# Mamba block, gated MLP and routed low-rank layer on one core: attention part moved forward in the step, norm rows turned by DMA, convolution read from PSUM

## The reference

```
h0  = LN(x)
a   = rmsnorm(h0) * ln1;  z, xBC, dt = a @ w_in.T
xBC = silu(causal depthwise conv of 4 taps over xBC + bias)        # x:128, B:128, C:4 x 128
dt  = softplus(dt + bias); chunks of 128 tokens, 4 heads: decayed scan (Mamba-2)
h1  = h0 + ((scan + D * x) * silu(z)) @ w_out.T
m   = h1 + (silu(h2 @ gate.T) * (h2 @ up.T)) @ down.T,  h2 = rmsnorm(h1) * ln2, 1792 inner channels
x1  = x + LN(m)
out = x1 + LN(u),  u = h3 @ W_up.T + low-rank term of the expert with the largest logit, h3 = LN(x1)
```

## Time and profile before

| | us |
|---|---|
| runs | 846.18, 846.56, 849.23; median 846.56 |
| profiled execution | 845.28, span 843.4 |
| PE busy, weight loads busy | 783.4 (93%), 552.9 (66%) |
| DVE, ACT, POOL busy | 488.4 (58%), 338.4 (40%), 148.7 (18%) |

### The profile page before, as it was taken

One profiled execution on the slowest core, in us unless ns is written; L12 is line 12 of the kernel. 1 busy time (PEld: TensorE's weight loads), 2 busy tenths in 40 slices (PEclk: granted clock), 3 DMA queues, 4 the chain that ended last, 5 costly groups with the idle time before them and its releaser, 6 DMA issues.

```text
span 843.4 us, 15200 instructions
## 1 busy us (share of the span) xinstructions
PE 783.4 (93%) x5712; PEld 552.9 (66%) x5726; DVE 488.4 (58%) x1123; ACT 338.4 (40%) x625; POOL 148.7 (18%) x198
## 2 busy tenths in 40 slices
PE   4987989899999999999999999999999999999944
PEld 3855855568657776678657776678656776677632
DVE  6877767676635764376635764476635764464343
ACT  2744667325522364225532364125532365122211
POOL 1412121012210141012210231012210231000000
PEclk9998999989999999999999999999999999999987
DMA  9930000000002000200002000200002000100010
GB/s 332 385 123 1 2 25 1 26 1 2 2 1 75 1 2 1 76 0 0 0 0 75 0 0 0 75 0 0 0 0 75 0 0 0 50 1 1 13 38 25
DMA packets 15556, 29.69 MB, mean 35 GB/s; under 512 B 1312, under 2 KB 1440, under 8 KB 15520
## 3 DMA queue, kind: packets, MB, share of 16 engines
q1 hardware_dynamic: 15520, 29.21, 9.8%
HBM read 25.01 MB, written 4.19 MB: 35 GB/s over the span
## 4 chain that ended last, share of the span: by engine, by line
PE 68%; issue 14%; DVE 9%; POOL 4%; ACT 3%; DMA 1%; SPq 0%; DVEq 0%; POOLq 0%; ACTq 0%
PE gu L1149 25%; PE wa L1149 21%; PE acc L1149 13%; PE wc L1149 6%; POOL y L411 2%; PE wa L1172 2%; DVE weights L806 1%; POOL ra L395 1%; DMA weights<-in_w_in 1%; DVE hn L835 1%; DVE weights L969 1%; DVE hn L843 1%; DVE sg L952 1%; DVE stats_a L821 1%; DVE h2t L946 1%
## 5 line engine op out<-in xcount | busy, mean ns | idle before, releaser
L1149 PE MATMUL gu<-h2t,weights 128*128 128x256 f16 x2688 | 314.6, 275 | 1.2 <-DVE h2t L946 1.2
L1149 PEld LDWEIGHTS gu<-h2t,weights 128*128 128x128 f16 x2688 | 261.8, 99 | 50.9 <-issue 15.0
L1149 PE MATMUL acc<-weights,act 128*128 128x512 f16 x672 | 164.6, 381 | 7.5 <-DVE act L957 7.5
L952 DVE SCALAR_TENSOR_TENSOR sg<-gu,bound,sg 128x256 f32<-128x256 f32 x112 | 53.6, 479 | 114.4 <-ACT sg L610 114.0
L610 ACT ACTIVATE sg<-gu,scale_inv 128x256 f32<-128x256 f32 x112 | 53.0, 473 | 150.1 <-PE gu L1149 150.0
L1149 PEld LDWEIGHTS acc<-weights,act 128*128 128x128 f16 x672 | 65.1, 98 | 65.2 <-DVE act L957 9.0
L620 ACT ACTIVATE act<-sg 128x256 f16<-128x256 f32 x112 | 46.6, 416 | 147.5 <-DVE sg L952 146.7
L1149 PE MATMUL wa<-ht,weights 128*128 128x256 f16 x912 | 105.7, 274 | 0.0
L1149 PEld LDWEIGHTS wa<-ht,weights 128*128 128x128 f16 x912 | 89.7, 98 | 16.9
L866 DVE SCALAR_TENSOR_TENSOR xbc<-conv_pad,conv_ws,xbc 128x256 f32<-128x256 f32 x144 | 67.2, 508 | 28.6 <-ACT conv_pad L545 19.2
L957 DVE TENSOR_TENSOR act<-sg,act 128x256 f16<-128x256 f32 x112 | 50.2, 448 | 54.8 <-ACT act L620 54.8
(11 more groups left out here) (189 smaller groups left out, 853.0 us busy)
## 6 DMA issues: line engine op xcount, KB each, us to landing
xa<-in_x SPq DMA_DIRECT2D x8, 512.0 KB, 3.5
weights<-in_x SPq DMA_DIRECT2D x8, 512.0 KB, 4.1
out_x<-h SPq DMA_DIRECT2D x16, 256.0 KB, 2.1
weights<-in_w_in SPq DMA_DIRECT2D x5, 512.0 KB, 6.7
weights<-in_w_down SPq DMA_DIRECT2D x3, 768.0 KB, 13.4
weights<-in_w_gate SPq DMA_DIRECT2D x2, 1024.0 KB, 11.9
weights<-in_w_up SPq DMA_DIRECT2D x2, 1024.0 KB, 13.8
weights<-in_w_gate SPq DMA_DIRECT2D x2, 768.0 KB, 14.3
```

The lines of the kernel that those rows point to most:

```text
L952: nc.vector.scalar_tensor_tensor(sg[:, f % 2], GU[f % 2][:, SEQ:2 * SEQ], up_to_act, sg[:, f % 2], ALU.mult, ALU.mult).then_inc(sem("prod_ ...
L1149: return nc.tensor.matmul(dst, left, right, start=start, stop=stop)
```

## The change

The tables are rewritten, so that part a starts earlier in its step. On PE:

```diff
-            A_AT = {1: lambda g: a_t1(g), 2: lambda g: a_in(g, 0), 3: lambda g: (a_in(g, 1), a_in(g, 2), a_dt(g)),
-                    4: lambda g: a_z(g, 0), 5: lambda g: (a_z(g, 1), a_tok(g)),
-                    6: lambda g: (a_dec(g, 0), a_dec(g, 1)), 7: lambda g: (a_att(g, 0), a_dec(g, 2)),
-                    8: lambda g: (a_att(g, 1), a_state(g)), 9: lambda g: (a_y(g, 0), a_y(g, 1)),
-                    10: lambda g: a_o(g, 0), 11: lambda g: a_o(g, 1), 13: lambda g: a_t2(g)}
-            C_AT = {4: lambda g: c_t3(g, 0), 5: lambda g: c_t3(g, 1), 6: lambda g: c_logits(g),
-                    7: lambda g: c_zt(g), 8: lambda g: c_u(g, 0), 9: lambda g: c_u(g, 1)}
+            A_AT = {0: lambda g: a_in(g, 1), 1: lambda g: (a_in(g, 2), a_dt(g)), 2: lambda g: a_z(g, 0),
+                    3: lambda g: (a_z(g, 1), a_tok(g)), 4: lambda g: (a_dec(g, 0), a_dec(g, 1)),
+                    5: lambda g: (a_att(g, 0), a_dec(g, 2)), 6: lambda g: (a_att(g, 1), a_state(g)),
+                    7: lambda g: (a_y(g, 0), a_y(g, 1)), 8: lambda g: a_o(g, 0), 9: lambda g: a_o(g, 1)}
+            NEXT_AT = {13: lambda g: a_in(g, 0)}
+            C_AT = {4: lambda g: alone(g) and (c_t3(g, 0), c_t3(g, 1)), 6: lambda g: c_logits(g),
+                    7: lambda g: c_zt(g), 10: lambda g: c_u(g, 0), 11: lambda g: c_u(g, 1)}
```

`NEXT_AT` holds work of the next group: its first input projection in block 13, on DVE its statistics, centring and lower half in blocks 8, 9 and 10, on ACT the upper half in block 10 and the first taps in block 13. On DVE:

```diff
-            A_AT = {1: lambda g: a_t1(g), 2: lambda g: a_conv(g, 0), 3: lambda g: (a_conv(g, 1), a_dtv(g)),
-                    4: lambda g: a_conv(g, 2), 5: lambda g: (a_dt(g), a_h0(g)),
...
+            A_AT = {0: lambda g: a_conv(g, 0), 1: lambda g: (a_conv(g, 1), a_dtv(g)),
+                    2: lambda g: (a_dt(g), a_conv(g, 2)), 3: lambda g: a_h0(g),
+                    5: lambda g: (a_dec(g, 0), a_dec(g, 1), a_att(g, 0)), 6: lambda g: a_att(g, 1),
+                    7: lambda g: (a_y(g, 0), a_y(g, 1)), 8: lambda g: a_h1(g, 0),
+                    9: lambda g: a_h1(g, 1), 10: lambda g: a_weight(g), 11: lambda g: a_lo2(g)}
+            NEXT_AT = {8: lambda g: a_stats(g), 9: lambda g: a_center(g), 10: lambda g: a_lo1(g)}
+            C_AT = {0: lambda g: c_stats1(g), 1: lambda g: c_x1(g), 3: lambda g: c_stats2(g), 4: lambda g: c_h3_lo3(g),
+                    6: lambda g: c_route(g), 12: lambda g: c_stats3(g), 13: lambda g: c_out(g)}
```

The three norms are no longer turned on PE, except those of group 0 and the last h3. ACT and DVE write f16 halves as rows, and SP turns them, 128 tokens with both halves (128x1024 f16, 256 KB) at a time, two transfers for each tensor:

```diff
+            def transposed(dst, rows, j, done):
+                sp.dma_start_transpose(dst[:, :, :, j * P:(j + 1) * P].rearrange("p s k q -> p (s k) q"),
+                                       rows[:, j].rearrange("p s d -> p (s d)")).then_inc(done, 16)
...
             def step(a, b, c):
+                following = a is not None and a + 1 < GROUPS
+                if following:
+                    a_x(a + 1)
+                if c is not None and not alone(c):
+                    c_t3(c)
+                if following:
+                    a_t1(a + 1)
+                if a is not None:
+                    a_t2(a)
                 if c is not None:
...
+                    c_store(c)
+                if b is not None:
+                    c_x(b)
+            a_x(1)
+            a_t1(1)
```

`h2t` becomes two tiles. The convolution's taps are read from PSUM, and ACT's copy to `conv_pad` goes away (group 0 keeps a copy for pairs 1 and 2):

```diff
-                            xbc[:, c], pad[:, c, k:k + SEQ], cw[:, c * TAPS + k:c * TAPS + k + 1],
-                            xbc[:, c], ALU.mult, ALU.add)
+                            xbc[:, c, late:], conv_in(g, c)[:, 0:SEQ - late], cw[:, c * TAPS + k:c * TAPS + k + 1],
+                            xbc[:, c, late:], ALU.mult, ALU.add)
```

So the PSUM banks rotate with the group, `a_z` waits for `conv_ready` of its pair, and `a_tok`, which writes over the third pair's products, waits for all six channel blocks:

```diff
             def a_tok(g):
                 pe.wait_ge(sem("xbc_ready"), g * 3 + 1)
-                pe.wait_ge(sem("dtv_ready"), g + 1)
+                pe.wait_ge(sem("conv_ready"), g * XBC + (2 if head(g) else XBC))
```

`wait_apart` is removed everywhere, and the hardware loop is replaced by steps written out:

```diff
-            with eng.Fori(2, GROUPS - 1) as i:
-                step(i + 1, i, i - 1)
...
+            for t in range(1, GROUPS + 2):
+                a, b, c = [g if 0 <= g < GROUPS else None for g in (t, t - 1, t - 2)]
+                step(a, b, c)
```

More of the change, by code:

```diff
@@ L169, in build @@
         ss = sb("sumsq", [P, 2, TILES])
-        h2t = sb("h2t", [P, 2, KB, SEQ], F16)
+        h2t = [sb(f"h2t_{n}", [P, 2, KB, SEQ], F16) for n in range(2)]
         h1b = sb("h1b", [P, TILES, D])
@@ L347, in _, with a_x, a_t1 @@
-            steps(sp, step)
+            def transposed(dst, rows, j, done):
+                sp.dma_start_transpose(dst[:, :, :, j * P:(j + 1) * P].rearrange("p s k q -> p (s k) q"),
+                                       rows[:, j].rearrange("p s d -> p (s d)")).then_inc(done, 16)
+            def a_x(g):
+                sp.wait_ge(sem("h0_ready"), g * 2)
+                sp.dma_start(xa[:], x_g[g]).then_inc(x_loaded, 16)
+            def a_t1(g):
+                sp.wait_ge(sem("z_ps_ready"), g * 2)
+                sp.wait_ge(sem("dt_ps_ready"), g)
+                for j in range(TILES):
+                    sp.wait_ge(sem("hn_split"), g * 2 + j - 1)
+                    transposed(ht, rows_1, j, ht_loaded)
@@ new lines, in a_t2, with c_x @@
+            def a_t2(g):
+                prev(g - 1, FBLK, FBLK, sp, sem("gu_ready"))
+                for j in range(TILES):
+                    sp.wait_ge(sem("h2_split"), g * 2 + j - 1)
+                    transposed(h2t[g % 2], rows_2, j, h2t_loaded)
+            def c_x(g):
+                if g > 0:
+                    sp.wait_ge(sem("out_ready"), g * 2)
+                if g == 0:
+                    wait_split(sp, order)
+                sp.dma_start(x1[:], x_g[g]).then_inc(xc_loaded, 16)
@@ L348, in _ @@
+            a_x(1)
+            a_t1(1)
+            steps(step)
             sp.wait_ge(stored, 16 * TILES * GROUPS)
@@ L483, in first @@
                 a_ce(0)
+                a_norm(1)
                 a_rms(0)
-                chain_a.close()
             first()
-            steps(pool, step)
+            steps(step)
         @block.scalar
@@ L621, in b_hi, with c_hi3 @@
                     .then_inc(sem("act_hi"), 1)
+            def c_hi3(g):
+                for j in range(TILES):
+                    eng.wait_ge(sem("h3_ready"), g * 2 + j + 1)
+                    nc.scalar.activation(rows_3[:, j, 0], h3[:, j], ACT.Copy).then_inc(sem("h3_hi"), 1)
             def c_t3(g, b):
-                eng.wait_ge(sem("h3t_ps_ready"), g * 2 + b + 1)
+                eng.wait_ge(sem("h3t_ps_ready"), b + 1)
                 prev(g, 2, 2, eng, sem("u_ps_ready"))
@@ L661, in step @@
                         C_AT[f](c)
+                    if a is not None and a + 1 < GROUPS and f in NEXT_AT:
+                        NEXT_AT[f](a + 1)
                 if a is not None:
@@ L690, in first @@
                 upper_halves(range(S_GU + 7, S_MIX))
+                a_hi1(1)
                 a_t2(0)
+                a_conv(1, 0)
                 chain_a.close()
             first()
-            steps(eng, step)
+            steps(step)
         @block.vector
@@ L1084, in step @@
                         C_AT[f](c)
+                    if a is not None and a + 1 < GROUPS and f in NEXT_AT:
+                        NEXT_AT[f](a + 1)
                 if a is not None:
-                    a_t2(a)
                     chain_a.close()
@@ L1142, in _ @@
             first()
-            steps(dve, step)
+            steps(step)
         @block.tensor
@@ L1446, in first @@
                 a_o(0, 0)
+                a_o(0, 1)
                 spread(2)
-                a_o(0, 1)
                 a_t2(0)
+                a_in(1, 0)
             first()
-            steps(pe, step)
+            steps(step)
 RING = 4
```

370 lines of the change are left out of this document (205 added, 165 removed).

## The result

The changed kernel takes 838.4 us (median), the kernel before 846.4 beside it: ratio 0.9886, with a 95% interval of 0.9864 to 0.9909. One execution of the changed kernel took 1624.7 us; it is in that median and left out of the ratio. The profiled execution took 837.98, with a span of 836.1. So it is 1.1% faster; the forecast said 835. Inside the loop, though, two of its terms were off, in opposite directions.

The account below looks back on a forecast made before the run. The prediction took a loop step to be PE's own work, plus what PE waits for. Loop -6, start and step 1 -3, step 8 and tail -0.9 made -10 on 845.3 us: 835, range 828 to 841, chance 0.46.

Parts of the forecast that it names:

- The wait of 2.3 at `a_tok`: In each step PE newly waits 2.3 us for the third convolution pair, behind log and dt; bounds nothing and 3.6.
- The rival that nothing waits there: At `a_tok`, dt or the log come sooner than added up, so no wait: 821 us; chance 0.16.
- Loop steps ... net -1.0: Loop steps and step 2, six in all: each loses 3.3 us of transposes and waits and gains 2.3 of waiting.
- The clock: PE's clock after a wait: no cost in the sum, as a row after 2.59 us idle took its full-clock 2.28.
- The rival that had the clock fall: At `a_tok`, a wait of 3.6 us and a lower clock costing 2.5 a step: 858 us; chance 0.12.
- the clock falls in the loop: A sign named in advance: the forecast is wrong if PE's clock falls in the loop.
- Loop in all: Loop steps and step 2, six at -1.0 us each: -6 us.
- The start and step 1: Before and in step 1: 1.7 us of transposes and 4 of waits go, 3 come: -3 us, bounds -7 and +6.
- The transfers: Turning transfers take T = 3 us each, bounds 2.1 and 9.9, and are hidden in loop steps below T = 4.
- the rival of slow transfers: Turning transfers beyond T = 4 make PE wait: some 875 us at T = 5, over 1050 at 9.9; chance 0.12.
- Step 8 and tail: After the loop: `h3t` 0.9 and routing wait 0.48 go, output of group 6 +1.8, increments -1.3; together -0.9 us.
- The last sum: -6 - 3 - 0.9 = -10 on the profiled 845.3 us, giving 835 to 836 from span or median too.

Follow-up runs that it names:

- e3_filler: The changed kernel with 18 products that nobody reads put on PE while it waits at `a_tok`: 831.0 us, ratio 0.9804.
- e8: The kernel before, with only its loop written out and the increments in DVE's and POOL's chains removed: 837.7 us, ratio 0.9879.
- e12_pair_first_from_sbuf: e1_pair_first with the third convolution pair's taps read from a copy that ACT makes in SBUF: 816.1 us, ratio 0.9629.
- e11_pair_first_increments: e1_pair_first with the increments back in DVE's chains: 817.3 us, ratio 0.9658.
- e2_increments_back: The changed kernel with the increments back behind the waits of DVE's chains, POOL's left away: 851.8 us, ratio 1.0049.
- e4_pair_from_sbuf: The changed kernel with the third pair's products copied to SBUF by ACT and DVE's taps reading them there: 866.4 us, ratio 1.0229.
- e5_transfers_twice: e1_pair_first with each turning transfer sent twice, one after another, each waited for on SP: 935.6 us in one execution.
- e1_pair_first: The changed kernel with the third convolution pair ahead of dt in DVE's block 2, nothing else: 815.2 us, ratio 0.9626.

## Why the prediction was right, and where it was wrong

- **The wait of 2.3 at `a_tok`: right.** 2.24 by the starts, from dt in 1.98 (2.0) and taps in 2.67 (2.7). The rival that nothing waits there (821) did not come true.
- **"Loop steps ... net -1.0": mis-sized.** Without the clock's part the step is 93.47 (486.46 to 579.93), 1.85 less. I counted the two waits by the page's brackets, 0.7; by starts they are 0.50 and 0.52, and behind the second stood another 0.39 inside the group, seen as 2.28 for a row that takes 1.88. Transposes, by starts, are 2.67. So 4.08 go and 2.24 come.
- **The clock: the step that failed.** The forecast's sum has nothing for it, since "after an idle time of 2.59 PE's next row took its full-clock 2.28". That was one place (granted clock 1.00). In the changed kernel a shorter idle time, 2.08, has both outcomes: five falls in seven, 8.35 us in all; e3_filler gives 7.4 of them back. The rival that had the clock fall had it only with a wait of 3.6, and counted from 3.3 on. One of the forecast's own signs of being wrong, "the clock falls in the loop", came true.
- **Loop in all:** six times -1.85 is -11.1; the clock's 8.35 and a wait of 0.87 that the missing input projection leaves at the end of step 7 make it -1.9, where the forecast had -6. One error was 5 us too shy, the other 9 us too hopeful. That the total came within 3 us of the forecast's -10 is luck in part: these two partly cancelled, and 2.3 us that no term had (1.4 in step 2, 0.9 in step 8 and the tail) made up for more.
- **The start and step 1: right**, -2.2 for -3, and 1.4 more in step 2, where the row at the lower clock has gone. The waits at the end of step 1 were 1.63 and 0.92 instead of 0.74 and 3.92, the row behind them fast; the transfers at the end of `first` cost 5.3 at the low clock.
- **The transfers: right.** They land in 3.2 to 3.3 (T = 3), and no loop step waits for them; the rival of slow transfers did not come true. The Trainium skill gives 1309 ns for a 128x128 block by DMA ("VectorE: DVE Perf Modes", on the three transpose paths). Eight blocks in one instruction landed after 3.2 us here, so that figure doesn't add up over blocks.
- **Step 8 and tail: -1.8 for -0.9.** By starts `h3t` and the wait for routing give 1.5 (0.9 and 0.5 in the sum), and the tail, from the last down product on, went from 33.5 to 33.2 where I had +0.5.
- **The last sum** says "835 to 836 by either". From the median of the runs, 846.6, the same -9.9 gives 836.7.
- **What the forecast did not ask**: which part of the gain comes from which edit. It gave the increments 1.2 a step inside `a_tok`'s sum (1.0 in dt, 0.2 in the taps) and 1.3 in the tail, and never priced them against the kernel before. There they alone were worth 1.2%, the whole gain. Moving part a, turning by DMA and reading from PSUM together brought 838.4 against 837.7, nothing: of e8's 94.23 a step, 24 transposes (2.67) and `hn`'s wait (0.36) go, 2.24 of waiting come, and 1.39 by the clock (8.35 over six). With the pair first only the 3.03 remain, 94.23 to 91.21, and the same work is worth 22 us.
- It also took DVE's order as given. Its own numbers showed the way out: the pair doesn't depend on dt, dt waits for the log 4.0 after `a_z(0)`, and the pair's products are ready before.

Left open: why the clock fell in five of seven equal places and not in the other two. And no run has the turning by DMA without the earlier start of part a: that the 3.03 a step are transposes and `hn`'s wait is read from rows. That reading from PSUM adds little once the pair stands first is shown by e12_pair_first_from_sbuf.

## What to carry to other kernels

On an in-order engine, ask of each pair of neighbouring entries which one's input comes first; work whose input is ready belongs in front of work that must wait, above all where another engine waits for the ready one. Price a wait on TensorE with the row behind it, read by starts and against the same row where nothing was late; here a stall of 2.24 us cost another 1.67 in five places of seven. And before crediting a large edit, run its small companions alone: here two removed lines are worth as much as the whole measured gain, and the large edit's own 22 us came out only when two names changed places.

## What the runs showed of the hardware

- An instruction that only increments a semaphore, behind a wait in a chain of small DVE operations, costs 0.11 us each time (0.20 against 0.31 from one to the next). In a chain off PE's path it cost nothing a step (e11_pair_first_increments: 91.20 against 91.21).
- Behind an idle time of 2.08 us PE's granted clock fell in five places of seven: 0.60 in the mean over 24 products of 128x256, which took 4.45 instead of 2.78. With products in between it did not fall. Behind 3.3 to 3.5 (e2_increments_back) it fell in five of seven too, behind 5.0 (e4_pair_from_sbuf) in all seven, and behind the one idle time of 2.59 in the kernel before it did not.
- A DMA that turns 256 KB of f16 from SBUF to SBUF lands after 3.2 to 3.3 us, when two are sent one behind the other, and two keep SP's queue busy for 2.6 us. Sent alone, it landed after 3.0 to 3.1 (e5_transfers_twice). Here is SP at block 5 of a step of the changed kernel (start, length, engine, line, operation):

```profile
401.32 2.61 SPq L357 DMA_TRANSPOSE h3t<-weights  x2
```

- Six taps with the products in PSUM take 2.67 us, beside POOL's products of two masks (the changed kernel) and without them (e1_pair_first). With the products in SBUF they take 2.91 when POOL is idle and 5.58 beside POOL's products.
